# Attention scores issued in groups that wait for all their PSUM banks first, with masks behind them, masks moved to GpSimd beside the expert work, and two moves in the opening

## The reference, cut to what matters

```
xn = layernorm(x)
x = x + mla_attention(xn) + experts(xn, top 4 of 8, clipped gate)   # layer 0
xn = layernorm(x)
x = x + sparsemax_attention(xn) + gqa_block(xn)                      # layer 1
# gqa_block = grouped attention, residual, rmsnorm, experts (top 2 of 8, silu)
```

## Time and profile before

| | |
|---|---|
| median of three runs | 3224.46 us |
| the profiled execution | 3229.72 us |
| its span (first to last instruction) | 3227.9 us |
| mean granted PE clock | 0.956 |
| PE busy | 2843.6 us, 88% |
| DVE busy | 2161.9 us, 67% |
| ACT busy | 1622.1 us, 50% |
| POOL busy | 1399.3 us, 43% |

### The profile page before, as it was taken

One profiled execution on the slowest core, in us unless ns is written; L12 is line 12 of the kernel. 1 busy time (PEld: TensorE's weight loads), 2 busy tenths in 40 slices (PEclk: granted clock), 3 DMA queues, 4 the chain that ended last, 5 costly groups with the idle time before them and its releaser, 6 DMA issues. The chain is left out here.

```text
span 3227.9 us, 61041 instructions
## 1 busy us (share of the span) xinstructions
PE 2843.6 (88%) x21398; PEld 2276.0 (71%) x21398; DVE 2161.9 (67%) x6229; ACT 1622.1 (50%) x3388; POOL 1399.3 (43%) x1941
## 2 busy tenths in 40 slices
PE   3877789999999999979888888898799999999986
PEld 1555578888888888856666666666588888888864
DVE  3876778678777767756777777766645544454576
ACT  1544444444444454445555555565455545545553
POOL 3587742343233233275556666322222222222377
PEclk8878899999999999989999999999899999999999
DMA  2465567678777777613333334210365555565445
GB/s 80 143 232 185 203 242 304 260 267 316 278 271 278 273 289 271 255 30 61 94 92 106 106 105 106 90 67 22 138 226 197 221 200 203 197 228 193 137 99 125
DMA packets 192067, 580.11 MB, mean 180 GB/s; under 512 B 22857, under 2 KB 144657, under 8 KB 157457
## 3 DMA queue, kind: packets, MB, share of 16 engines
q1 hardware_dynamic: 154896, 525.03, 44.1%
q0 software_dynamic: 36864, 51.14, 7.7%
HBM read 450.14 MB, written 125.96 MB: 178 GB/s over the span
## 5 line engine op out<-in xcount | busy, mean ns | idle before, releaser
L1128 POOL TENSOR_TENSOR al<-t,ah 128x512 fp32r<-128x512 f32 x220 | 285.6, 1298 | 989.4 <-ACT ah L1350 989.4
L579 PE MATMUL bank<-masks_bf,ident_bf 128*128 128x128 bf16 (+1 forms) x2304 | 581.2, 252 | 113.9 <-DVE st L1800 52.8
L533 PE MATMUL bank<-xh,gu 128*128 128x256 f32 x3520 | 628.3, 285 | 10.0 <-issue 5.1
L1800 DVE TENSOR_REDUCE st<-bank 128x1 f32<-128x512 f32 (+3 forms) x1024 | 422.2, 480 | 202.3 <-PE bank L586 202.1
L1447 ACT ACTIVATE pt<-bank 128x512 f32<-128x512 f32 (+1 forms) x1152 | 511.4, 540 | 91.2 <-PE bank L589 89.7
L533 PEld LDWEIGHTS bank<-xh,gu 128*128 128x128 f32 x3520 | 505.2, 190 | 19.6 <-issue 13.5
L579 PEld LDWEIGHTS bank<-masks_bf,ident_bf 128*128 128x128 bf16 x2304 | 225.6, 98 | 391.6 <-DVE st L1800 112.6
L586 PE MATMUL bank<-ksT,qsT 128*128 128x512 f32 (+3 forms) x1536 | 438.1, 382 | 0.0
L589 PE MATMUL bank<-qaT,ksT 128*128 128x512 f32 (+3 forms) x1536 | 435.3, 392 | 0.0
L1455 ACT ACTIVATE oT<-bank 128x512 f32<-128x512 f32 x192 | 114.4, 596 | 547.9 <-PE bank L658 547.9
L533 PE MATMUL bank<-xl,gu 128*128 128x256 f32 x1760 | 352.5, 282 | 0.0
(11 more groups left out here) (253 smaller groups left out, 5124.7 us busy)
## 6 DMA issues: line engine op xcount, KB each, us to landing
gu<-wu_scratch SPq DMA_DIRECT2D x110, 2056.0 KB, 7.9
dn<-wd_scratch SPq DMA_DIRECT2D x110, 1024.0 KB, 9.5
xs<-xs_scratch SPq DMA_DIRECT2D x110, 264.0 KB, 9.0
ys_scratch<-yb SPq DMA_DIRECT2D x110, 256.0 KB, 9.8
raw<-in_gu SPq DMA_DIRECT2D x16, 1024.0 KB, 5.6
wu_scratch<-hi SPq DMA_DIRECT2D x16, 1024.0 KB, 9.5
wu_scratch<-lo SPq DMA_DIRECT2D x16, 1024.0 KB, 12.8
xs_scratch<-empty SPq DMA_DIRECT2D x32, 264.0 KB, 5.3
```

The lines of the kernel that those rows point to most:

```text
L533: mm = pe.matmul(bank[:, TS * h:TS * (h + 1)], gu[:, col:col + P], x[s % 2][:, TS * k:TS * (k + 1)], start=(n == 0), stop=(n == len(terms) ...
L579: pe.matmul(bank[:, diag:diag + P * len(unit)], ident_bf[:, :], masks_bf[:, 0 if which == "q" else 1, 0:len(unit), :].rearrange("p n k -> ...
L1128: pool.tensor_tensor(em["al"][s % 2][:, m, :], em["t"][g % 2][:, :], em["ah"][s % 2][:, m, :].bitcast(F32), ALU.subtract).then_inc(al_read ...
L1800: ins = dve.reduce_max(st[:, 0, r:r + 1], bank[:, first:first + width], AX.X)
```

## The change

Five edits:

1. `scores` issues units in groups: of three where the ring has three banks, of two where it has four. All waits for the banks of a group stand in front of its first matmul; then the scores of all its units, then the masks, each as the last matmul of its unit. `s_full` moves from the scores to the mask.
2. For the k scores of pairs with experts (`bare`) there is no mask at all. POOL sets the forbidden half of each diagonal block of pt to 0 after the exponentials (`clear`, two AFFINE_SELECT of 128x256 elements for each head, four a pair), and `outputs` waits for POOL's `pt_ready` there and no more for ACT. `PT_AT` is reordered so that two diagonal blocks lie together.
3. `clear(G, 0)` stands in POOL's order between expert part 1 and part 2, `clear(G, 1)` between part 2 and part 3.
4. The 128 router scatters are spread over the same pairs 3 to 18 in counts of 4 to 12 (`FIRST_SCATTERS`) and not eight in each.
5. `norm_heads(0, slice(4, H))` moves on DVE from ahead of pair 0 to behind the maxima and the shift of pair 1.

```diff
+FIRST_SCATTERS = (10, 5, 5, 10, 10, 8, 10, 5, 5, 5, 5, 10, 12, 12, 12, 4)
-PT_AT = {0: 0, 3: 512, 1: 640, 2: 1024}
+PT_AT = {0: 0, 2: 512, 3: 768, 1: 896}
...
                     mem = mems[kinds[G // NP]]
-                    for u in units:
-                        name = (which, G, u)
-                        S.add(name, "dve" if which == "q" else "act")
-                        if S.former[name]:
-                            pe.wait_ge(*S.former[name])
-                        bank = S.bank(name)
...
+                    bare = which == "k" and G in plan
+                    side, width_of = 0 if which == "q" else 1, Q_UNITS if which == "q" else K_UNITS
+                    size = 3 if len(S.banks) == 3 else 2
+                    for group in [units[i:i + size] for i in range(0, len(units), size)]:
+                        for u in group:
+                            S.add((which, G, u), "dve" if which == "q" else "act")
+                            if S.former[(which, G, u)]:
+                                pe.wait_ge(*S.former[(which, G, u)])
+                        for u in group:
+                            bank, unit = S.bank((which, G, u)), width_of[u]
+                            for n, (j, blk, first, width) in enumerate(unit):
+                                end = bare and n == len(unit) - 1
+                                ks = mem["ksT"][key_at[G] % 2][j]
...
+                            if bare:
+                                mm.then_inc(s_full, 1)
+                        for u in group if not bare else ():
+                            bank, unit = S.bank((which, G, u)), width_of[u]
+                            diag = min(first + (P * blk if which == "q" else 0) for _, blk, first, _ in unit)
+                            pe.matmul(bank[:, diag:diag + P * len(unit)], ident_bf[:, :],
+                                      masks_bf[:, side, 0:len(unit), :].rearrange("p n k -> p (n k)"),
+                                      start=False, stop=True, skip_group_check=True).then_inc(s_full, 1)
...
-                    pe.wait_ge(s_act, S.count[("k", G, NU - 1)])
+                    if G in plan:
+                        pe.wait_ge(pt_ready, 4 * (1 + sorted(plan).index(G)))
+                    else:
+                        pe.wait_ge(s_act, S.count[("k", G, NU - 1)])
...
+                def clear(G, j):
+
+                    pt = mems[kinds[G // NP]]["pt"]
+                    pool.wait_ge(s_act, S.count[("k", G, NU // 2 * (j + 1) - 1)])
+                    for first, size in ((0, 1024), (768, 256)):
+                        blocks = pt[:, j, first:first + size].rearrange("p (n q) -> p n q", n=2)[:, :, 0:P]
+                        pool.affine_select(out=blocks, in_=blocks, pattern=[[0, 2], [1, P]], compare_op=ALU.is_ge, fill=0.0,
+                                           base=0, channel_multiplier=-1).then_inc(pt_ready, 1)
...
                     if G in plan:
-                        for q in range(2, 6):
+                        clear(G, 0)
+                        experts(G, 2)
+                        clear(G, 1)
+                        for q in range(3, 6):
                             experts(G, q)
...
+                    if G == 0 and is_at(0, "mla"):
+                        norm_heads(0, slice(4, H))
...
-                if kinds[0] == "mla":
-                    norm_heads(0, slice(4, H))
```

More of the change, by code:

```diff
@@ L477, in pipeline @@
         per_batch = 16 * NT * CHOICES[0]
-        scatter_at = {2 * b + 3 + half: [(b, half)] for b in range(B) for half in range(2)} if em else {}
+        scatters = [(b, t, k) for b in range(B) for t in range(NT) for k in range(CHOICES[0])]
+        scatter_at = {3 + i: scatters[sum(FIRST_SCATTERS[:i]):sum(FIRST_SCATTERS[:i + 1])]
+                      for i in range(len(FIRST_SCATTERS))} if em else {}
         def routes(G, lag):
@@ new lines, in scores @@
+                    bare = which == "k" and G in plan
[11 more added lines that the diff above has]
+                                ks = mem["ksT"][key_at[G] % 2][j]
+                                if which == "q":
+                                    mm = pe.matmul(bank[:, first:first + width], mem["qsT"][:, P * blk:P * (blk + 1)],
+                                                   ks[:, 0:width], start=(n == 0), stop=end, skip_group_check=True)
+                                else:
+                                    mm = pe.matmul(bank[:, first:first + width], ks[:, P * blk:P * (blk + 1)],
+                                                   mem["qaT"][:, T - width:T], start=(n == 0), stop=end,
+                                                   skip_group_check=True)
+                            if bare:
[6 more added lines that the diff above has]
+                                      start=False, stop=True, skip_group_check=True).then_inc(s_full, 1)
@@ L1254, in route_std, with route_scatter @@
                     pool.tensor_tensor(small[:, 4:8], small[:, 0:4], minus_half[:, 0:NT], ALU.pow).then_inc(r_std, 1)
[L1256 to L1265, removed]
+                def route_scatter(b, t, k):
+                    if t == 0 and k == 0:
+                        pool.wait_ge(r_rows, NT * (b + 1))
+                        pool.wait_ge(r_w, b + 1)
+                        pool.wait_ge(r_slot, b + 1)
+                    where = bass.IndirectOffsetOnAxis(slots[0][:, NT * b + t, k:k + 1], 0)
+                    pool.indirect_dma_start(xs_dram, where, ro["rows"][b % 4][:, t, :], None).then_inc(scattered[b % 4], 16)
                 row_std(0)
@@ L1302, in _ @@
                         route_std(G // 2 + 1)
-                    for b, half in scatter_at.get(G, ()):
-                        route_scatter(b, half)
+                    for b, t, k in scatter_at.get(G, ()):
+                        route_scatter(b, t, k)
                     if is_at(n - 1, "gqa") and p == 3:
```

3 lines of the change are left out of this document (2 added, 1 removed).

## The result

The changed kernel takes 3351.2 us (median of four runs, 3343.9 to 3354.6) against 3222.8 (3217.6 to 3225.3) of the kernel before: a ratio of 1.039, with a 95% interval of 1.037 to 1.041. That is 128 us slower, where 75 were forecast, above the 3262 to 3330 that were given for this mechanism, and a little above the 3350 at which the whole range ended.

The account below looks back on a forecast made before the run. It took the alone pairs' closed chain through PE, DVE and ACT, without slack, as deciding. Terms +97 + 9 - 25 + 5 - 9 - 5 - 7 + 10 = +75 us on 3227.9 gave 3300 us, range 3250 to 3350.

Parts of the forecast that it names:

- Alone pairs: Pairs 50 to 137: groups lengthen both score links, 1.1 us a pair over 88 pairs, +97 us.
- the closed sum without slack: Alone pair: links 2.32 + 1.24 + 3.07 + 1.99 = 8.62 us, so what lengthens a link lengthens the pair.
- Rival A: Alone pairs have slack: a pair loses 0.2 us, 3207 us; or PE-bound there, 3155; chance 0.12 for both.
- clean pair: Alone pair whose links follow with no other wait between; forecast to grow by 1.25 us, 0.8 to 1.45.
- DVE starts at about 0.77: Alone pairs, q scores: four pieces ahead of the first signal take 0.48 us, making DVE 0.19 us late.
- Tail: The 15 tail pairs, where POOL is close to the pace itself: groups cost 0.6 us each, +9 us.
- Layer 1: Layer 1's expert stage: 0.87 us saved a pair, 0.65 to 0.75 lost waiting for three banks; -9 us.
- Layer 0: Layer 0's expert stage, PE-bound: cheaper scores give -25 us, later `low` behind POOL's selects +5, 0 to 15.
- rival C: Alone pairs: the clock falls with the new holes, some +60 us, 3350 to 3360 us; chance 0.09.
- Select: POOL's AFFINE_SELECT in `clear`: taken at 0.7 us, hidden up to 1.1 us each in layer 1.
- rival B: AFFINE_SELECT on POOL is slow: at 2 us `outputs` waits in layer 1, +70 us, 3370 us; chance 0.07.
- Opening: Pairs 0 to 20: norm_heads moved -5 us, scatters evened out -7, groups +10.

Follow-up runs that it names:

- e3: Changed kernel with groups only in pairs with experts, alone pairs issuing unit by unit as before; 3246.4 us, ratio 1.0017 to the kernel before.
- e9: Kernel of e6 with groups of two for the q scores of alone pairs only; ratio 1.0104 to the kernel before.
- e10: Kernel of e6 with groups of two for the k scores of alone pairs only; ratio 1.0041 to the kernel before.
- e12: Kernel of e6 with each alone-pair unit on its own, its mask behind its own scores; ratio 0.9905 to the kernel before.
- e2: Changed kernel without groups: old loop over units, masks first, none on bare k scores; 3209.3 us, ratio 0.9898 to the kernel before.
- e5: The kernel before, run and traced again with the second set of experiments; 3240.0 us.
- e6: Kernel of e2 with POOL's first clear moved from ahead of expert part 2 to behind it; 3197.7 us, ratio 0.9871 to the kernel before.
- e1: Kernel before with the groups alone, all masks kept and no other part of the change; 3417.9 us, ratio 1.0543 to the kernel before.
- e8: Kernel before with the new spread of the router scatters alone; ratio 1.0000 to the kernel before.
- e7: Kernel before with the move of norm_heads alone; ratio 0.9991 to the kernel before.
- e11: Kernel of e6, old order in each unit, but alone pairs wait for two units' banks in front of the first; ratio 1.0059 to the kernel before.
- e4: Changed kernel with each unit's bank wait just ahead of its own scores, masks still behind the group; 3283.9 us, ratio 1.0138 to the kernel before.

## Why the prediction was right, and where it was short

**Alone pairs (forecast +97, measured +103).** The mechanism was right: the closed sum without slack, the last group of each kind waiting for two banks, DVE's third maximum and ACT's second exponential as releasers. Rival A, slack in the alone pairs, is excluded by the 103 themselves, and e3, e9 and e10 show that they are the groups'. A clean pair grew by 1.52 where 1.25 was forecast with an upper end of 1.45. The step that was mis-sized is the first signal of a q group: "DVE starts at about 0.77", but it starts at 1.02. The four pieces were counted by their columns, with the loads hidden. How far exposed loads make the difference is not shown; e12 shows that the mask behind the scores costs 0.21 by itself even in a group of one. The q link grew 0.95 against 0.55 (0.65 at most), the k link 0.86 against 0.7, and 0.25 came back in the evictions behind. Pairs that are not clean passed less on, so the mean of 1.17 a pair lies near the 1.1 that was taken: two errors of opposite sign met in the sum, which is luck.

**Tail (+9, measured +13).** "0.6 each" was too low by a third, so POOL hid less than was assumed. The same waits stand there: 13.9 us for DVE's top and 10.6 for ACT's pt.

**Layer 1 (-9, measured +9).** Each item was a little off, all the same way. The bare k scores saved 0.37 for three units and not 0.40, which with the loads behind them came to 0.68 net a pair in e2 where 0.80 was forecast. The wait for three banks costs 0.9 in a clean pair by PE's starts and not 0.65 to 0.75: DVE's half takes 1.68 and PE starts 0.15 behind it as forecast, but PE would have been there 0.92 behind DVE's start (2681.80 + 1.43 against 2682.31), where it was 1.22 in the earlier trace rows and 1.1 in the forecast. And the last mask of a q group leaves 0.08 of load time exposed ahead of the expert matmuls. Groups of three cost 0.82 a pair (e3 against e2), more than the 0.68 that was gained.

**Layer 0 (-20, measured +4).** The saved matmul time was nearly as forecast: 0.77 us in a median pair, some 22 in all against 25. The step that failed is that it was booked in full, less "+5 in all, 0 to 15" at `down`, with nothing for the clock (only rival C had it, for the alone stretch) and nothing for other waits. PE's waits in the stage, of the changed kernel:

```profile
PE bank L556 <- issue: 21.0, 15, 2.6
...
PE bank L556 <- ACT yb L1385: 7.8, 12, 0.7
...
PE bank L510 <- DMA xs<-xs_scratch: 4.3, 9, 0.8
```

Before, these rows were 13.6, 3.9 and 0.3. All waits at `down` grew by 12 us, those for DMA xs and for DVE's both and st by some 8; and 34 us were at the lower clock where 17 had been (20.5 in e5), worth some 7 to 8. With the 22 saved that makes +5. Of the 12 us at `down` nearly 8 are the holes at the six places, in e2 too. e6 got 4.4 of them back from the selects' place and some 5 from the clock; the rest is there because PE now arrives 0.6 earlier. The longer waits for ACT's yb come with the groups (2.7 in e2, 9.6 in e1); by which path is open.

**Select (0.7 assumed, 0.41 measured).** It is quicker even than the 0.6 taken for a COPY of its size, so rival B is out by far: `outputs` waited for POOL nowhere in layer 1. Its price was in the place it took in POOL's order.

**Opening (-2, measured -4).** This is right by the sum, but not by its parts, so by luck. The scatters bring nothing (e8), norm_heads at most a few us (e7). The groups alone made an opening of 460 us in e1, 31 above e5's, where the changed kernel shows no loss (their clocks were 0.80 and 0.85). Only single traces stand for the openings, and those of e9, e10 and e11 differ too (436, 444, 448), with groups or waits in it but with norm_heads and scatters moved. Whether these edits cover the groups' cost, or the clock or a chance order on POOL does, stays open.

**Rival C** did not come: the alone stretch has a clock of 0.95 against 0.96. The fall that did come was in layer 0's stage.

## What to carry to other kernels

Issue work in groups only where the consumer is not waiting: in front of an engine that is the pace, a wait for several buffers costs the time until the last of them, and a signal moved behind other work delays the consumer, here by 0.44 us at the first maximum of a pair. Here the waits were worth 45 to 58 us of some 930 (e11, e4), what stays without them 38 (e4), and the costs of the q and the k groups added up. Where a new short piece of work is put on a helper engine, its length matters less than what stands right behind it in that engine's order: moving 0.77 us of selects out from between a 5.4 us power and the operation that TensorE waits for was worth 10 us in layer 0's stage, and the same move nothing in layer 1's. And a saving on the busiest engine should be booked only after asking which waits it will merely lengthen: of some 22 us of saved matmul time in layer 0's stage (0.77 in a median pair) 4 arrived in e2, and 14 once the order on POOL was mended.

## What the runs showed of the hardware

- AFFINE_SELECT on POOL took 0.41 us for 128x256 float32, two in a row 0.77.
- A row of float32 scores is not always quicker than one with masks between. In the clean pair the second q score starts 0.36 us behind the first in the old form, although a mask stands between them, and 0.45 behind it in a group, with nothing between; the first one's 512 columns are 0.21 us at 2.4 GHz. In the k group of the same pair it is 0.34. What decides this is open. The Trainium skill (TensorE: Matmul & The Clock Gate, section "Step-by-step: what each phase is for") says that loads can be pulled ahead of running matmuls. The second load started 0.23 us behind the first matmul's start in the q group and 0.11 in the k group, both inside that matmul's row, which agrees; it doesn't tell the two apart.
- In layer 0's stage holes of 2.5 us on an otherwise full PE were followed in four of six cases by 3.4 us at the lower clock (e2), holes of 1.8 in one of six (e6), holes of 1.2 in none of six (the kernel before).
